# A chunked state scan in a decoder layer: the state's inputs are made by GpSimd from the scaled x instead of by VectorE from PSUM

## The chip, the core and the metric

The kernel runs on one core of a Trainium2 chip. The metric is the device time of one execution in microseconds (us). Three runs of the kernel before gave 635.28, 635.28 and 643.08 us, with a median of 635.28 us.

The engines are named as in the profile: PE is TensorE's matmul and PEld its weight load, DVE is VectorE, ACT is ScalarE, POOL is GpSimd, SP is the queue that issues DMAs.

## The reference, cut to what matters

A pre-norm decoder layer on x of shape 2 x 1024 x 256: a Mamba-2 block with a memory pool, then cross-attention, then a routed feed-forward with 8 experts. The change is inside the Mamba-2 scan, whose recurrence per head (8 heads of 64 columns, state width 128) is

```python
dt = jax.nn.softplus(dt + dt_bias)
A = -jnp.exp(A_log)
dA = jnp.exp(dt * A)
dtx = dt[..., None] * xs
def step(h, inp):
    dA_t, dtx_t, B_t, C_t = inp
    h = h * dA_t[:, :, None, None] + dtx_t[..., None] * B_t[:, None, None, :]
    y = jnp.einsum('bhpn,bn->bhp', h, C_t)
    return (h, y)
y = jnp.moveaxis(ys, 0, 1) + D_param[None, None, :, None] * xs
y = _rmsnorm(y * jax.nn.silu(z), gnorm_w)
```

## The kernel before, in words

The kernel is one program with five hand-written instruction streams, one for each engine. Each stream is in order, and the streams meet only at semaphores. The two batch rows make 2048 tokens, cut into 16 chunks of 128 tokens. Input projections, convolution and gates come first, then the scan over the 16 chunks, then scoring and the memory pool, cross-attention, and the experts.

The scan does not step token by token. For a chunk t it needs:

- G, the products of B and C inside the chunk (128 x 128), masked to the causal part: `gmat`;
- the decay between each pair of tokens for each head (128 x 8 x 128): ACT clamps and exponentiates it into `lmat`, and POOL multiplies it by G (`make_m`, L475, which signals `m_ready`);
- x scaled by dt, `xdt` (128 tokens x 512 columns), for the part of y that stays in the chunk (PE, L1760);
- x scaled by dt and by the decay to the chunk's end, `xend` (128 x 512), from which PE makes what the chunk adds to the state (L1764, into bank 6).

All of these have two buffers, picked by the parity p of the chunk. The steps of one chunk by stream, with t running from 1 to 14 in the steady part:

- PE, `pe_step(t)`: turns chunk t+1 from columns into rows with PE transposes into banks 0 and 1 (L1719 to L1721; it waits for `sides_ready`, since VectorE reads those banks), then `mix(t)`: the part of y from the earlier state (L1756; it waits for `state_added`), the part inside the chunk (L1760; it waits for `m_ready`), the addition to the state (L1764). Then it projects the gated y of chunk t-1 (L1775) and sums its squares (L1768).
- DVE, `dve_step(t)`: `chunk_sides(t+1)` copies B (L1166), masks G (L1169, signals `g_ready`), and makes `xdt` and `xend` from the same PSUM bank 0 (L1176, two instructions of one line; the second signals `sides_ready`). Then `sum_y(t)` (L1186, L1190), `add_state(t)` (L1195; it waits for PE's product and for POOL's decay), and `gate(t)`: four instructions that add D times x (L1200, both inputs in SBUF), and one that multiplies by the gate (L1207, both inputs in SBUF).
- POOL, `step(t)`: `decay_state(t)` multiplies the state by the chunk's decay (L484; it waits for `inter_mm` and `state_added`), `make_m(t+1)` (L475; waits for `decay_mat` and `g_ready`), `sum_squares(t-1)` (L489, L491).
- ACT: clamp (L697, eight instructions), exponential (L702), squares (L741), the residual (L753), and eviction of the output (L746, L748), each for its chunk.
- SP: for each chunk three loads: the chunk's columns (L367), the rows of cumulated decay (L373), the exponentials of those (L381).

Before the steady part DVE clamps chunk 0 and 1 itself (`clamp`, L1148). In the first `chunk_sides`, between `xdt` and `xend`, stand three more things: `clear_first` (L1153), the clamp of chunk 1, and `finish_decays`, which waits for ACT's last exponential (L737), clears entries of `dec` and multiplies `wend` by dt (L1158). ACT makes the exponential of `wend` in L736. PE's transposes of chunk 1 wait for `sides_ready` of chunk 0.

Of the kernel before, what the change touches and what calls it, by code (L numbers as in the profile page):

```python
# [10 lines left out]
ALU = mybir.AluOpType  # L11
ACT = mybir.ActivationFunctionType
AX = mybir.AxisListType.X
ds = bass.ds
# [9 lines left out]
DI, NS, H, HP = 512, 128, 8, 64  # L24
# [16 lines left out]
    "eps_set", "past_cleared", "ln_var_1", "rstd_1_1", "rstd_2_1", "rms_var_1", "rstd_3_1", "rstd_4_1",  # L41
    "ln_var_2", "rstd_1_2", "rstd_2_2", "rms_var_2", "rstd_3_2", "rstd_4_2", "dt_kept", "dt_steps_1",
    "dt_steps_2", "dt_abs", "dt_sum", "dt_ready", "cum_rows_kept", "cum_kept", "tot_kept", "wend_diff", "d_cols_set_1", "d_cols_set_2",
    "first_cleared_1", "first_cleared_2", "decay_ready", "gn_rstd_1", "ones_bf_set_1", "gn_rstd_2", "w2b_ready", "pos_ready", "cols_set", "mask_row_ready", "iotas_ready", "ln3_var", "ln3_rstd",
    "hot_ready", "prefix_ready", "held_ready", "block_expert_ready", "rows_found",
)
ACT_EVENTS = (
# [15 lines left out]
def events_of(name):  # L63
    return next(events for events in (DVE_EVENTS, ACT_EVENTS, POOL_EVENTS, PE_EVENTS) if name in events)


def at(name):

    return events_of(name).index(name) + 1


def build(nc, a, out):
# [3 lines left out]
    with ExitStack() as ctx:  # L76
# [5 lines left out]
        def sem(name):  # L82
            if name not in names:
                names[name] = ctx.enter_context(nc.semaphore(name))
            return names[name]


        dve_once, act_once, pool_once, pe_once = sem("dve_once"), sem("act_once"), sem("pool_once"), sem("pe_once")
        met = []

        def reached(name):
            met.append(name)
            events = events_of(name)
            assert [m for m in met if m in events] == list(events[:at(name)])
            return 1
# [18 lines left out]
        def cut(shape):  # L114
            n = int(np.prod(shape))
            v = arena[:, place[0]:place[0] + n]
            place[0] += n
            if len(shape) == 2:
                v = v.rearrange("p (a b) -> p a b", a=shape[0])
            if len(shape) == 3:  # L120
                v = v.rearrange("p (a b c) -> p a b c", a=shape[0], b=shape[1])
            return v
# [17 lines left out]
        xdt = cut([2, DI])  # L140
        xend = cut([2, DI])
# [32 lines left out]
        dt_v, dta, cum, dec = (dts[:, i, :] for i in range(4, 8))  # L174
        wend = dt_raw
        cum_rows, ecum_rows = dt_neg, dt_pos

        def th(v):
            return v.rearrange("p (t h) -> p t h", h=H)

        def heads(v, n):

            return v.unsqueeze(2).broadcast_to([P, H, n])
# [152 lines left out]
        S = sem  # L336
# [110 lines left out]
        def _(pool):  # L447
# [21 lines left out]
            pool.wait_ge(S("conv_done"), NX * NBLK)  # L469
            pool.memset(state, 0.0).then_inc(pool_once, reached("state_set"))  # L470

            def make_m(t, p):
                pool.wait_ge(S("decay_mat"), t + 1)
                pool.wait_ge(S("g_ready"), t + 1)
                pool.tensor_tensor(lmat[:, p, :, :], lmat[:, p, :, :],  # L475
                                   gmat[:, p, :].unsqueeze(1).broadcast_to([P, H, P]), ALU.mult
                                   ).then_inc(S("m_ready"), 1)

            def decay_state(t):

                pool.wait_ge(S("inter_mm"), t + 1)
                pool.wait_ge(S("state_added"), t)
                sv = state.rearrange("p (h n) -> p h n", h=H)
                pool.tensor_tensor(sv, sv, heads(dec[:, ds(t * H, H)], HP), ALU.mult).then_inc(S("state_decayed"), 1)  # L484

            def sum_squares(t, p):

                pool.wait_ge(S("sq_ready"), t + 1)
                pool.tensor_tensor(sq[:, p, 0:2, :], sq[:, p, 0:2, :], sq[:, p, 2:4, :], ALU.add).then_inc(S("sq_part"), 1)  # L489
                pool.wait_ge(S("sq_part"), t + 1)  # L490
                pool.tensor_tensor(sq[:, p, 0, :], sq[:, p, 0, :], sq[:, p, 1, :], ALU.add).then_inc(S("sq_summed"), 1)  # L491

            pool.wait_ge(pool_once, at("state_set"))
            make_m(0, 0)
            make_m(1, 1)
            pool.wait_ge(dve_once, at("first_cleared_2"))
            decay_state(0)

            def step(t, p):

                decay_state(t)
                make_m(t + 1, 1 - p)
                sum_squares(t - 1, 1 - p)
            step(1, 1)
            with pool.Fori(1, NT // 2 - 1) as i:
                step(2 * i, 0)
                step(2 * i + 1, 1)
# [70 lines left out]
            for n in range(NT // 2):  # L578
                pool.wait_ge(S("upd_ready"), n + 1)
                pool.wait_ge(S("res_y_added"), n + 1)  # L580
                xv = xres[:, 2 * n:2 * n + 2, :].rearrange("p a d -> p (a d)")
# [8 lines left out]
            with pool.Fori(0, NT // 2) as i:  # L590
                for p in range(2):
                    t = 2 * i + p
# [441 lines left out]
        def _(dve):  # L1034
# [110 lines left out]
            def clamp(t):  # L1145
                dve.wait_ge(S(f"cum_loaded{t}"), 16)
                for h in range(H):
                    i = dve.tensor_scalar(lmat[:, t, h, :], cum_all[:, t, h, :], cum[:, t * H + h:t * H + h + 1], 0.0, ALU.subtract, ALU.min)  # L1148
                i.then_inc(S("clamped"), 1)

            def clear_first():
                dve.wait_ge(act_once, at("ecum_exp"))
                dve.memset(ecum_rows[TB * H:TB * H + H, :], 0.0).then_inc(dve_once, reached("first_cleared_1"))  # L1153

            def finish_decays():
                dve.wait_ge(act_once, at("dec_exp"))
                dve.memset(th(dec)[:, 0:NT:TB, :], 0.0).then_inc(dve_once, reached("first_cleared_2"))
                dve.tensor_tensor(wend, wend, dt_v, ALU.mult).then_inc(dve_once, reached("decay_ready"))  # L1158
                dve.wait_ge(dve_once, at("decay_ready"))

            def chunk_sides(t, p, wait):

                dve.wait_ge(S("g_mm"), t + 1)
                if wait:
                    dve.wait_ge(S("state_mm"), t - 1)
                dve.tensor_copy(b_tok[:, p, :], bank[1][:, 0:P])  # L1166
                if wait:
                    dve.wait_ge(S("m_ready"), t - 1)
                dve.tensor_tensor(gmat[:, p, :], bank[1][:, P:2 * P], tri_le[:, :], ALU.mult).then_inc(S("g_ready"), 1)  # L1169
                xv = bank[0][:, :].rearrange("p (h n) -> p h n", h=H)  # L1170
                for dst, col in ((xdt, dt_v), (xend, wend)):
                    if dst is xend and isinstance(t, int) and t == 0:
                        clear_first()
                        clamp(1)
                        finish_decays()
                    i = dve.tensor_tensor(dst[:, p, :].rearrange("p (h n) -> p h n", h=H), xv, heads(col[:, ds(t * H, H)], HP), ALU.mult)  # L1176
                i.then_inc(S("sides_ready"), 1)

            def sum_y(t, p, first=False):
                yv = y_in[:, p, :, :]  # L1180
# [27 lines left out]

            clamp(0)
            chunk_sides(0, 0, False)  # L1210
            chunk_sides(1, 1, False)
            dve.wait_ge(S("conv_done"), NX * NBLK)
            sum_y(0, 0, True)
# [3 lines left out]
            def dve_step(t, p, wait=True):  # L1217
                chunk_sides(t + 1, 1 - p, True)
                sum_y(t, p)
                add_state(t)  # L1220
                gate(t, p, wait)
# [1044 lines left out]
```

## Time and profile before

| | |
|---|---|
| Runs | 635.28, 635.28, 643.08 us |
| Profiled execution: its own time, its span | 640.2 us, 638.5 us |
| PE busy | 584.8 us (92% of the span) |
| DVE busy | 393.2 us (62%) |
| ACT busy | 325.7 us (51%) |
| POOL busy | 171.6 us (27%) |
| Chain that ended last, by engine | PE 65%, DVE 19%, issue 7%, ACT 6% |

The profile comes from one execution of its own, with the time in the second row. Busy times are summed over the whole span. The chain that ended last is followed back from the last instruction, at each step to what released it. "Issue" is time for which the profile shows no wait. An engine's share over the whole span says little of one stage; the scan is the stretch from about 90 to 198 us.

### The profile page before, as it was taken

What the parts mean: (1) busy time and instruction counts of PE and PEld (TensorE: products, weight loads), DVE (VectorE), ACT (ScalarE), POOL (GpSimd) and SP (SyncE); (2) the same over time, 40 slices, a digit from 0 to 9 for tenths busy, and PEclk for the clock granted to TensorE, in tenths of its full rate; (3) what the DMA queues carried; (4) which work ended last, traced back from release to release, by engine and by line L of the source; (5) the groups of instructions that cost most, each with busy time, mean ns of one, the idle gap of its engine ahead of it and who ended that gap; (6) DMA issues with size and microseconds to landing.
All of it is one profiled execution on the core that took longest, in us unless ns stands there. A gap on an engine that the chain in (4) does not pass through costs nothing.

```text
span 638.5 us, 14059 instructions
## 1 busy us (share of the span) xinstructions
PE 584.8 (92%) x4820; PEld 462.1 (72%) x4821; DVE 393.2 (62%) x953; ACT 325.7 (51%) x708; POOL 171.6 (27%) x189
## 2 busy tenths in 40 slices
PE   7999998899988898987999999997599999999995
PEld 5444457677776565555788888886589999999994
DVE  4986798999997762555555566553744444444431
ACT  3887986777876413256566655554123322233220
POOL 0300016767673301741000000001212223322221
PEclk9999999999999679999999999998799999999998
DMA  8100126564532930008000000005711111111100
GB/s 257 43 1 0 46 81 191 151 193 156 169 127 78 394 136 4 1 1 263 12 19 11 18 18 19 10 18 126 247 26 35 34 32 31 35 40 34 28 17 0
DMA packets 47276, 49.50 MB, mean 78 GB/s; under 512 B 7607, under 2 KB 41627, under 8 KB 47227
## 3 DMA queue, kind: packets, MB, share of 16 engines
q1 hardware_dynamic: 41882, 43.65, 21.1%
q0 software_dynamic: 2208, 5.14, 2.9%
q8 instruction: 29, 0.48, 0.3%
q10 hardware_dynamic: 3136, 0.07, 0.3%
q14 instruction: 21, 0.16, 0.1%
HBM read 39.24 MB, written 5.26 MB: 70 GB/s over the span
## 4 chain that ended last, share of the span: by engine, by line
PE 65%; DVE 19%; issue 7%; ACT 6%; DVEq 1%; DMA 1%; POOL 1%; POOLq 0%; ACTq 0%
PE banks L2190 13%; PE banks L2201 12%; PE banks L1660 7%; DVE arena L1200 4%; PE banks L2043 4%; DVE arena L1176 3%; PE banks L2068 3%; PE banks L1944 3%; PE banks L2073 2%; PE banks L2086 2%; DVE arena L1125 2%; PE banks L2082 2%; PE banks L1955 2%; DVE ybuf L1417 2%; DVE arena L1186 1%
## 5 line engine op out<-in xcount | busy, mean ns | idle before, releaser
L1006 ACT ACTIVATE prob_b<-banks,gate_w 128x128 f32<-128x128 f32 x92 | 26.3, 368 | 115.5 <-PE banks L2190 115.5
L2201 PE MATMUL banks<-arena,prob_b 128*128 x368 | 83.1, 379 | 0.0
L2190 PE MATMUL banks<-ybuf 128*128 128x128 f32 x560 | 78.6, 275 | 0.0
L2201 PEld LDWEIGHTS banks<-arena,prob_b 128*128 128x128 f32 x368 | 68.2, 190 | 8.4
L2190 PEld LDWEIGHTS banks<-ybuf 128*128 128x128 f32 x560 | 72.1, 192 | 1.1
L1660 PE MATMUL banks<-featT,ybuf 128*128 128x512 f32 x160 | 70.2, 594 | 1.1 <-ACT featT L650 1.1
L1660 PEld LDWEIGHTS banks<-featT,ybuf 128*128 128x128 f32 x160 | 29.8, 190 | 36.6 <-issue 35.0
L1417 DVE TENSOR_REDUCE ybuf<-banks 128x12 f32<-128x1848 f32 (+1 forms) x32 | 46.1, 1441 | 15.7 <-PE banks L2043 15.7
L614 POOL DMA_INDIRECT out<-featT,dts x23 | 23.4, 1017 | 120.4 <-DVE featT L1606 120.4
L1125 DVE SCALAR_TENSOR_TENSOR arena<-arena,conv_w 128x512 f32<-128x512 f32 x72 | 48.9, 745 | 11.0 <-ACT arena L664 11.0
L594 POOL TENSOR_TENSOR xres<-xres,ybuf 128x256 f32 x16 | 11.6, 726 | 137.9 <-DVE ybuf L1437 137.9
L1584 DVE TENSOR_SCALAR prob_b<-banks,gate_w 128x128 f32<-128x128 f32 x92 | 26.0, 344 | 31.1 <-PE banks L2190 31.0
L475 POOL TENSOR_TENSOR arena<-arena 128x1024 f32<-128x1024 f32 x16 | 37.9, 2367 | 18.9 <-DVE arena L1169 10.3
L697 ACT ACTIVATE arena<-arena,dts 128x128 f32<-128x128 f32 x112 | 34.3, 389 | 6.5 <-DMA arena<-cum_rows 5.6
L2190 PE MATMUL banks<-ybuf,w_out 128*128 128x128 f32 x176 | 34.0, 275 | 0.0
L948 ACT ACTIVATE prob_b<-banks 122x2048 f32<-122x2048 f32 x16 | 30.1, 1879 | 7.1 <-PE banks L2068 7.1
L1775 PEld LDWEIGHTS banks<-w_out,arena 128*128 128x128 f32 x128 | 23.5, 190 | 12.8 <-DVE arena L1207 7.9
L1775 PE MATMUL banks<-w_out,arena 128*128 128x256 f32 x128 | 30.9, 384 | 1.6 <-DVE arena L1207 1.6
L1591 DVE COPY ybuf<-arena 128x1024 f32 x23 | 16.0, 697 | 26.6 <-PE banks L2190 25.3
L607 POOL DMA_INDIRECT xres<-x_rows,dts x23 | 23.8, 1034 | 23.9 <-DVEq L1564 17.2
L1423 DVE TENSOR_TENSOR arena<-arena,banks 128x512 f32<-128x512 f32 x16 | 11.0, 690 | 30.8 <-PE banks L2056 30.8
L2043 PE MATMUL banks<-arena 32*128 32x154 f32 x512 | 25.9, 314 | 4.4 <-DVE ybuf L1417 1.1
(354 smaller groups left out, 1240.1 us busy)
## 6 DMA issues: line engine op xcount, KB each, us to landing
arena<-cum_rows SPq DMA_DIRECT2D x16, 512.0 KB, 4.5
arena<-W1T SPq DMA_DIRECT2D x8, 1024.0 KB, 11.7
arena<-W2T SPq DMA_DIRECT2D x8, 1024.0 KB, 11.1
arena<-arena SPq DMA_DIRECT2D x16, 320.0 KB, 3.3
featT<-ecum_rows SPq DMA_DIRECT2D x30, 128.0 KB, 3.0
xres<-x SPq DMA_DIRECT2D x4, 512.0 KB, 11.2
x_rows<-xres SPq DMA_DIRECT2D x16, 128.0 KB, 2.2
ybuf<-attn_in_wT SPq DMA_DIRECT2D x1, 1288.0 KB, 7.0
```

The costliest lines, as they stand in the source:

```text
L475: pool.tensor_tensor(lmat[:, p, :, :], lmat[:, p, :, :], gmat[:, p, :].unsqueeze(1).broadcast_to([P, H, P]), ALU.mult).then_inc(S("m_ready ...
L697: i = act.activation(lmat[:, p, h, :], cum_all[:, p, h, :], ACT.Relu, bias=cum[:, ds(t * H + h, 1)], scale=-1.0)
L948: act.activation(prob_m[0:KM, :, :, :].rearrange("p h g n -> p h (g n)"), quad[0:KM, :, :], ACT.Exp).then_inc(S("prob_m_ready"), 1)
L1006: i = act.activation(hidT[:, p, f, :], bank[2 * p + 1][:, (f - 4) * P:(f - 3) * P], ACT.Relu, bias=b1_cols[:, ds(e * NFF + f, 1)])
L1125: i = dve.scalar_tensor_tensor(acc, raws[j][:, g, k:k + BLK], conv_w[:, g, k:k + 1], acc, ALU.mult, ALU.add)
L1417: dve.tensor_reduce(for_part.rearrange("p g h -> p h g"), quad[:, :, 0:n * LK].rearrange("p h (g n) -> p h g n", g=n), AX, ALU.max).then_i ...
L1584: i = dve.tensor_scalar(hidT[:, p, f, :], bank[2 * p][:, f * P:(f + 1) * P], b1_cols[:, ds(e * NFF + f, 1)], 0.0, ALU.add, ALU.max)
L1660: m = pe.matmul(in_bank(kind, n)[:, :], w_in[:, k, f * P:(f + 1) * P], featT[:, k, blk * BLK:(blk + 1) * BLK], start=(k == 0), stop=(k == ...
L1775: m = pe.matmul(bank[7][:, 0:D], gated[:, p, k, :], w_out[:, k, :], start=(k == 0), stop=(k == NZ - 1))
L2043: m = pe.matmul(quad[:, h, i * LK:(i + 1) * LK], qT[r, t % 3, g0 + i, :], keys[r, t // TB, g0 + i, :], start=True, stop=True)
L2190: m = pe.matmul(bank[2 * p + half][:, f * P:(f + 1) * P], w1_now[k][p][:, (4 * half + f) * P:(4 * half + f + 1) * P], xsT[:, p, k, :], sta ...
L2201: m = pe.matmul(bank[4 + p][:, 0:D], hidT[:, p, f, :], w2_of[:, ds(e * NFF + f, 1), :].rearrange("p a n -> p (a n)"), start=(f == 0), stop ...
```

## The change

`xend` is no longer made by VectorE. VectorE makes only `xdt` from PSUM, and signals `sides_ready` after it. GpSimd gets a new function `end_inputs(t, p)`, which multiplies `xdt` (SBUF) by `wend` (SBUF) into `xend`. So `wend` stays the bare decay, and the instruction that multiplied it by dt is gone. GpSimd's new instruction stands in its stream directly before `make_m` of the same chunk, and PE's product from `xend` keeps its place behind the wait for `m_ready`. In the first chunks the three things between `xdt` and `xend` now stand between `chunk_sides(0)` and `chunk_sides(1)`.

```diff
+            def end_inputs(t, p, wait=True):
+                pool.wait_ge(S("sides_ready"), t + 1)
+                if wait:
+                    pool.wait_ge(S("state_mm"), t - 1)
+                pool.tensor_tensor(xend[:, p, :].rearrange("p (h n) -> p h n", h=H), xdt[:, p, :].rearrange("p (h n) -> p h n", h=H),
+                                   heads(wend[:, ds(t * H, H)], HP), ALU.mult)
...
             pool.wait_ge(pool_once, at("state_set"))
+            pool.wait_ge(act_once, at("dec_exp"))
+            end_inputs(0, 0, False)
             make_m(0, 0)
+            end_inputs(1, 1, False)
             make_m(1, 1)
...
                 decay_state(t)
+                end_inputs(t + 1, 1 - p)
                 make_m(t + 1, 1 - p)
                 sum_squares(t - 1, 1 - p)
...
                 dve.memset(th(dec)[:, 0:NT:TB, :], 0.0).then_inc(dve_once, reached("first_cleared_2"))
-                dve.tensor_tensor(wend, wend, dt_v, ALU.mult).then_inc(dve_once, reached("decay_ready"))
-                dve.wait_ge(dve_once, at("decay_ready"))
...
-                for dst, col in ((xdt, dt_v), (xend, wend)):
-                    if dst is xend and isinstance(t, int) and t == 0:
-                        clear_first()
-                        clamp(1)
-                        finish_decays()
-                    i = dve.tensor_tensor(dst[:, p, :].rearrange("p (h n) -> p h n", h=H), xv, heads(col[:, ds(t * H, H)], HP), ALU.mult)
-                i.then_inc(S("sides_ready"), 1)
+                dve.tensor_tensor(xdt[:, p, :].rearrange("p (h n) -> p h n", h=H), xv, heads(dt_v[:, ds(t * H, H)], HP), ALU.mult
+                                  ).then_inc(S("sides_ready"), 1)
...
             chunk_sides(0, 0, False)
+            clear_first()
+            clamp(1)
+            finish_decays()
             chunk_sides(1, 1, False)
```

## Rows read from the trace of the kernel before

**Rows 1.** Stages view, the steady part; busy us and instructions of each engine, granted clock.

```profile
103.94:194.50 90.56, 82.13 (x605) 65.01 (x601) 86.05 (x169) 67.87 (x174) 66.09 (x56) 1.00 0.52 159
```

**Rows 2.** Chain of waits in the scan: start us, us, engine and line.

```profile
113.45 2.95 DVE arena L1200 x4
...
194.50 0.69 DVE arena L1186
```

**Rows 3.** Groups of POOL, steady part: idle before, with what ended it.

```profile
L475 POOL TENSOR_TENSOR arena<-arena 128x1024 f32<-128x1024 f32 x14 | 33.1, 2366 | 13.3 <-DVE arena L1169 7.5 <-ACT arena L702 5.8
L484 POOL TENSOR_TENSOR arena<-arena,dts 128x512 f32<-128x512 f32 x14 | 17.3, 1234 | 10.7 <-PE banks L1756 10.7
```

**Rows 4.** Timeline from 101.5 to 107.6 us, DVE: start us, us, line, count.

```profile
101.56 0.69 DVE L1195 TENSOR_TENSOR arena<-arena,banks 128x512 f32<-128x512 f32 x1 [1.09 <-POOL arena L484]
102.16 1.13 DVE L1200 SCALAR_TENSOR_TENSOR arena<-arena,d_cols 128x128 f32<-128x128 f32 x4
...
103.33 0.69 DVE L1207 TENSOR_TENSOR arena<-arena 128x512 f32<-128x512 f32 x1
103.94 0.28 DVE L1166 COPY arena<-banks 128x128 f32<-128x128 f32 x1
104.34 1.28 DVE L1176 TENSOR_TENSOR arena<-banks,dts 128x512 f32<-128x512 f32 x2
106.92 0.68 DVE L1195 TENSOR_TENSOR arena<-arena,banks 128x512 f32<-128x512 f32 x1
```

**Rows 5.** Timeline from 111.5 to 117.2 us, POOL and DVE.

```profile
111.54 2.37 POOL L475 TENSOR_TENSOR arena<-arena 128x1024 f32<-128x1024 f32 x1 [0.77 <-ACT arena L702]
113.37 3.02 DVE L1200 SCALAR_TENSOR_TENSOR arena<-arena,d_cols 128x128 f32<-128x128 f32 x4
113.87 0.79 POOL L489 TENSOR_TENSOR featT<-featT 128x256 f32<-128x256 f32 x1
114.73 0.46 POOL L491 TENSOR_TENSOR featT<-featT 128x128 f32<-128x128 f32 x1
115.15 1.10 POOL L484 TENSOR_TENSOR arena<-arena,dts 128x512 f32<-128x512 f32 x1
116.52 0.69 DVE L1207 TENSOR_TENSOR arena<-arena 128x512 f32<-128x512 f32 x1
```

**Rows 6.** Timeline, one clamp of chunk 1 on DVE and the POOL instruction beside it.

```profile
92.90 2.39 POOL L475 TENSOR_TENSOR arena<-arena 128x1024 f32<-128x1024 f32 x1 [2.88 <-ACT arena L702]
92.99 2.37 DVE L1148 TENSOR_SCALAR arena<-arena,dts 128x128 f32<-128x128 f32 x1
```

**Rows 7.** Timeline, two meetings of the gate multiply and the state's decay.

```profile
122.27 1.04 POOL L484 TENSOR_TENSOR arena<-arena,dts 128x512 f32<-128x512 f32 x1 [0.90 <-PE banks L1756]
122.29 1.57 DVE L1207 TENSOR_TENSOR arena<-arena 128x512 f32<-128x512 f32 x1 [0.24 <-DVE arena L1200]
...
128.94 0.69 DVE L1207 TENSOR_TENSOR arena<-arena 128x512 f32<-128x512 f32 x1 [0.24 <-DVE arena L1200]
128.94 1.59 POOL L484 TENSOR_TENSOR arena<-arena,dts 128x512 f32<-128x512 f32 x1 [0.92 <-PE banks L1756]
```

**Rows 8.** Timeline of the start of the scan: PE, DVE and POOL.

```profile
96.45 0.63 PE L1719 MATMUL banks<-ident,arena 128*128 128x128 f32 x4 [0.60 <-DVE arena L1176]
...
97.65 0.28 DVE L1169 TENSOR_TENSOR arena<-banks,tri_le 128x128 f32<-128x128 f32 x1
98.08 2.37 POOL L475 TENSOR_TENSOR arena<-arena 128x1024 f32<-128x1024 f32 x1 [2.80 <-DVE arena L1169]
100.39 1.06 POOL L484 TENSOR_TENSOR arena<-arena,dts 128x512 f32<-128x512 f32 x1
```

**Rows 9.** Waits of PE, 100 to 195 us: us in total, times, longest.

```profile
PE banks L1756 <- DVE arena L1195: 8.7, 10, 1.5
```

**Rows 10.** Stages view, two stretches after the scan, columns as in rows 1.

```profile
220.00:235.00 15.00, 14.22 (x69) 9.17 (x68) 8.13 (x36) 1.76 (x5) 0.00 (x0) 0.65 0.60 239
245.00:255.00 10.00, 7.55 (x45) 4.70 (x44) 1.21 (x5) 3.74 (x11) 2.56 (x14) 0.97 0.04 6
```

More of the change, by code:

```diff
@@ L43 @@
     "dt_steps_2", "dt_abs", "dt_sum", "dt_ready", "cum_rows_kept", "cum_kept", "tot_kept", "wend_diff", "d_cols_set_1", "d_cols_set_2",
-    "first_cleared_1", "first_cleared_2", "decay_ready", "gn_rstd_1", "ones_bf_set_1", "gn_rstd_2", "w2b_ready", "pos_ready", "cols_set", "mask_row_ready", "iotas_ready", "ln3_var", "ln3_rstd",
+    "first_cleared_1", "first_cleared_2", "gn_rstd_1", "ones_bf_set_1", "gn_rstd_2", "w2b_ready", "pos_ready", "cols_set", "mask_row_ready", "iotas_ready", "ln3_var", "ln3_rstd",
     "hot_ready", "prefix_ready", "held_ready", "block_expert_ready", "rows_found",
```

## The prediction

> **What bounds the kernel now.** I read the stages first, then the chain of waits through the scan, then the timeline of single chunks. In the steady part of the scan DVE is busy 86.05 of 90.56 us, PE 82.13, ACT 67.87 and POOL 66.09, at the full granted clock [rows 1]. The chain of waits runs through DVE's lines chunk after chunk [rows 2], and PE waits for DVE's add to the state 10 times, 8.7 us in all [rows 9]. So DVE sets the pace. The 14 frames from DVE's copy at 103.94 us [rows 4] to its instruction at 194.50 us [rows 2] take 90.56 us, 6.47 us each. A frame is DVE's work from one chunk's copy (L1166) to the next's.
>
> Busy time hides the next point: part of DVE's busy time is waiting inside an instruction. Take a frame with POOL out of the way, pieced together from rows 4. Copy to the scaled x is 104.34 - 103.94 = 0.40 us; copy to the add to the state (L1195) 106.92 - 103.94 = 2.98; that add to the first of the four skip instructions (L1200) 102.16 - 101.56 = 0.60; those four 103.33 - 102.16 = 1.17; the gate multiply (L1207) to the next copy 103.94 - 103.33 = 0.61. The sum is 2.98 + 0.60 + 1.17 + 0.61 = 5.36 us. Measured is 6.47, so 1.11 us a frame is lost to something, and DVE's recorded waits are too small to hold it.
>
> The timeline shows what it is lost to. The four L1200 take 3.02 us in one frame [rows 5] instead of 1.13 [rows 4], and their end follows POOL's instructions: POOL runs L475 until 113.91, L489 until 114.66, L491 until 115.19, L484 until 116.25, back to back, and the four end at 116.39, 0.14 us after the last. Between two POOL instructions one L1200 gets through, no more. Alone it is seen where a DVE clamp that begins 0.09 us after a POOL instruction takes 2.37 us and ends with it [rows 6]. Both directions occur [rows 7]: the gate multiply that starts 0.02 us after the state's decay takes 1.57 instead of 0.69 us; where both start together POOL takes 1.59 instead of 1.04 and DVE nothing extra. What reads PSUM is not held: the adds and products of PSUM with SBUF run in 0.68 us beside POOL in rows 4. So a DVE instruction with two SBUF inputs waits until the POOL instruction in progress is over.
>
> The SBUF — State Buffer page of the Trainium skill (section Who interferes with whom) says this outright: two SBUF inputs on DVE contend with GpSimd, the first holds the pair for its whole instruction, and at most one SBUF input does not contend. By that rule the new POOL instruction disturbs none of the PSUM steps beside it, and the sum below stays as it is; the trace agrees (0.68 us beside L475).
>
> **The change, part by part.**
>
> *DVE loses one instruction a frame.* The two L1176 become one; they take 1.28 us together and one alone 0.68 [rows 4], so DVE gains 0.60 us. All its later steps of the frame come 0.60 earlier: the first L1200 is ready 2.98 + 0.60 - 0.60 = 2.98 us after the copy.
>
> *POOL gets one instruction.* Nothing in the trace multiplies this very pair on POOL. The nearest is L484, the same shape and the same kind of broadcast column, 1.04 to 1.10 us where undisturbed [rows 5, 7, 8]; I take 1.06. Below it the bound is DVE's 0.68 for the same elements, above it 1.59, L484 held up. What reads PSUM on DVE lies beside it, so it isn't held. The GPSIMD Engine Reference of the Trainium skill (section 3.1) measures a two-input GpSimd multiply at 1.96 times DVE's; an estimate from it is 0.68 x 1.96 = 1.33 us, 0.27 more a frame, and the sum would be about 4 us higher. The row decides: 1.06.
>
> *The decay matrix product (L475) moves back.* This is what costs. Before, it waited for the masked G (end of L1169), or for ACT; from G's end to its start is 98.08 - 97.93 = 0.15 us [rows 8]. Now its queue holds the new instruction, which waits for the scaled x. In the new frame: scaled x ends at 0.40 + 0.68 = 1.08; the new instruction runs 1.23 to 2.29; L475 starts 0.06 before its forerunner's recorded end, as L484 does in rows 8, at 2.23, and with 2.37 us ends at 4.60. The first L1200 is ready at 2.98 and is held for 1.62 us. Before, with G's end at about 0.48, L475 could be over at about 3.0, and the first L1200 at 3.58 missed it.
>
> *After that every POOL instruction meets one L1200.* POOL's next three all have their inputs: the squares of the chunk before (that gate multiply ended at the frame's start), and the decay, which needs PE's product from the state (released by L1195 at about 3.1, over by about 4.6). So they run back to back as in rows 5. There, from L475's end to the gate multiply is 116.52 - 113.91 = 2.61 us. The gate multiply starts at 4.60 + 2.61 = 7.21, the next copy at 7.21 + 0.61 = 7.82 us. POOL waits for the next scaled x by then, so the frame repeats: its decay ends at about 7.0, and its next input comes at 7.82 + 1.23 = 9.05.
>
> *The sum of frames.* 14 x 7.82 = 109.5 us. In the last frame no decay follows the squares, and the last L1200 goes free: less 0.9. That leaves 108.6 against 90.56: +18.0 us.
>
> *The start.* PE's transposes of chunk 1 waited 0.60 us for DVE's second multiply of chunk 0 [rows 8]; that wait goes, and DVE's copy of chunk 1 comes 0.60 earlier, at 96.84. POOL then runs: new instruction 98.08 to 99.14 (scaled x ends at 97.93), L475 until 101.45, decay until 102.45. DVE's first add to the state waits for that decay already, 1.09 us [rows 4]; it now starts at about 102.56 instead of 101.56: +1.0 us. The new wait for ACT's last exponential and the product for chunk 0 lie ahead of chunk 1, and PE needs that product only after its own transposes; the deleted small multiply of `wend` and the clamp of chunk 1, which now runs before POOL is busy, are hidden by PE's weight products. I cost them at nothing; that cover is over 2 us of PE work, and if it were gone about 1 us would show.
>
> *Other queues.* Bank 0 comes free sooner, which PE can't use: it waits for L1195 in any case. On PE, chunk t+1's inside product starts after L475 at 4.6 instead of following the state's product at once, and its addition to the state ends near 6.8; DVE's next L1195 wants it at 7.82 + 2.38 = 10.2. ACT has 5.3 us of work in 7.82. SP's loads have more time than now. None becomes late.
>
> In all +18.0 + 1.0 = +19.0 us. Against the profiled execution's 640.2 that is 659.2; it stands 4.9 above the median, which I take as the base: 635.3 + 19.0 = **654 us**.
>
> **Rivals.**
>
> *DVE slips through.* The first L1200 gets its reads in before or within L475, or the new order leaves a gap. Then DVE keeps its 0.60 us and its old collisions: 6.47 - 0.60 = 5.87, near POOL's own work, 1.06 + 2.37 + 0.73 + 0.5 + 1.08 = 5.7. That gives 14 x -0.60 + 1.0 = -7.4 us, 628. For it: POOL is idle for 13.3 and 10.7 us before its two large instructions [rows 3], room for 14 new ones on paper. Against it: the meetings in [rows 5 to 7], where nothing got through. It decides if L475 ends before 2.98, so the new instruction would have to be no longer than zero. Chance 0.07.
>
> *Only the first L1200 is held.* It loses 1.62 us but the later ones lose no more than the old 1.11: 6.47 - 0.60 + 1.62 = 7.49 less the 0.4 or so that the decay took from the gate multiply, about 7.1. Then 14 x 0.63 + 1.0 = +9.8, 645, within 2%. For it: the decay sometimes starts with DVE [rows 7]. Against it: with L1195 far ahead, the decay isn't waiting for PE. Chance 0.12.
>
> *PE's clock falls.* PE idles about 1.2 us a frame more. The granted clock was 0.65 in a stretch where half was spent at 1.2 GHz, but 0.97 in one with PE busy 7.55 of 10 us [rows 10]; the new scan would have it busy 5.87 of 7.82, the same 75%. At the lower level 5.87 us of PE work a frame would be up to 11.7; three or four such frames add some 14 us: 668. Chance 0.06.
>
> **How the numbers follow.** Forecast 0.75. Its own range is 647 to 661: 14 frames with the new instruction at 0.68 (-5) or at 1.33 to 1.59 (+4 to +7), and the base between the runs. The range that holds 8 in 10 takes in most of the second rival below and something of the clock above: 644 to 664. Differences under 2%, 12.7 us, can't be told from no change here. Slower by over that (above 648): most of the forecast and all of the clock's case, 0.78; within: 0.18; faster: 0.04, as the first rival's 628 is itself within 2% and only its lower end is not.
>
> **What would show it.** A frame of about 7.8 us on DVE; L1200 at about 1.0 us an instruction (the four take some 4.1 us); POOL's new line at about 1.06 us; L475 starting about 2.2 us after DVE's copy; L484 no longer waiting for PE. It is wrong if L475 is over before the first L1200 starts, if L1200 runs in 0.35 us while L475 is in progress, or if PE's granted clock in the scan is under 1.

## The result, and the profile after

The kernel after takes 655.46 us (median of 4 runs, 653.38 to 657.43), against 635.28 us before. The ratio is 1.0307, 95% interval 1.0265 to 1.0349: 3.1% slower. The forecast was 654 us.

The profiled execution took 653.38 us, with a span of 651.6 us. The stages view of its steady part, with the columns of [rows 1], and the part after the scan:

```profile
105.15:214.31 109.16, 88.60 (x612) 66.65 (x610) 102.45 (x156) 67.90 (x174) 78.48 (x70) 0.98 0.42 126
214.31:651.60 437.29, 400.77 (x3868) 342.33 (x3868) 227.71 (x601) 178.57 (x382) 92.20 (x114) 0.97 0.19 62
```

The same 14 frames now take 109.16 us instead of 90.56 [rows 1]: +18.6. They begin at 105.15 instead of 103.94 us: +1.2. The scan thus ends 19.8 us later, close to the difference of the medians, 20.2 us. (The two spans differ by 13.1 only. The rest is after the scan: 437.29 us here, 444.00 before, with the same instructions at a mean granted clock of 0.97 against 0.96.)

Groups of the steady part, DVE then POOL; L1204 is now the skip instructions, L1211 the gate multiply, L1180 the scaled x, L476 the new multiply, L482 the decay matrix product, L491 the state's decay, L496 and L498 the sums of squares:

```profile
L1204 DVE SCALAR_TENSOR_TENSOR arena<-arena,d_cols 128x128 f32<-128x128 f32 x56 | 50.5, 960 | 0.0
L1180 DVE TENSOR_TENSOR arena<-banks,dts 128x512 f32<-128x512 f32 x14 | 9.5, 679 | 0.0
```

```profile
L482 POOL TENSOR_TENSOR arena<-arena 128x1024 f32<-128x1024 f32 x14 | 33.0, 2357 | 0.0
L491 POOL TENSOR_TENSOR arena<-arena,dts 128x512 f32<-128x512 f32 x14 | 15.2, 1082 | 6.6 <-PE banks L1763 5.2 <-issue 1.4
L476 POOL TENSOR_TENSOR arena<-arena,dts 128x512 f32<-128x512 f32 x14 | 14.6, 1042 | 24.2 <-DVE arena L1180 24.2
```

DVE is busy 102.45 us, 16.4 more, though it has one instruction a frame less. The 56 skip instructions are 50.5 us of it, 0.96 us each; free they take 0.35. POOL's two waits of [rows 3] have become one: 24.2 us ahead of L476, for the scaled x. L482 never waits. L491 still waits for PE, but only in the first two frames, 5.2 us in all.

One steady frame, DVE and then POOL, start and length in us:

```profile
121.01 0.28 DVE L1175 COPY arena<-banks 128x128 f32<-128x128 f32 x1
121.41 0.68 DVE L1180 TENSOR_TENSOR arena<-banks,dts 128x512 f32<-128x512 f32 x1
123.40 0.68 DVE L1199 TENSOR_TENSOR arena<-arena,banks 128x512 f32<-128x512 f32 x1
124.00 3.32 DVE L1204 SCALAR_TENSOR_TENSOR arena<-arena,d_cols 128x128 f32<-128x128 f32 x4
127.56 1.48 DVE L1211 TENSOR_TENSOR arena<-arena 128x512 f32<-128x512 f32 x1 [0.24 <-DVE arena L1204]
128.97 0.28 DVE L1175 COPY arena<-banks 128x128 f32<-128x128 f32 x1
```

```profile
122.27 1.04 POOL L476 TENSOR_TENSOR arena<-arena,dts 128x512 f32<-128x512 f32 x1 [2.15 <-DVE arena L1180]
123.28 2.36 POOL L482 TENSOR_TENSOR arena<-arena 128x1024 f32<-128x1024 f32 x1
125.59 0.78 POOL L496 TENSOR_TENSOR featT<-featT 128x256 f32<-128x256 f32 x1
126.45 0.46 POOL L498 TENSOR_TENSOR featT<-featT 128x128 f32<-128x128 f32 x1
127.45 1.04 POOL L491 TENSOR_TENSOR arena<-arena,dts 128x512 f32<-128x512 f32 x1 [0.55 <-issue]
```

L482 starts 2.27 us after the copy and ends at 125.64. The first skip instruction of that frame by itself:

```profile
124.00 1.78 DVE L1204 SCALAR_TENSOR_TENSOR arena<-arena,d_cols 128x128 f32<-128x128 f32 x1
```

It starts at 124.00, is ready to work for 1.64 us while L482 runs, and ends at 125.78, 0.14 us after it. The frame closes at 7.96 us; in this one the gate multiply, not the last skip instruction, is what meets L491. Over 13 frames, copy to copy, the mean is 7.86 us against 6.49 before.

### The profile page after: what moved, and what is told of

Read it like the earlier page. It is cut to its first block, busy times and chain, and to the rows that moved or that the text cites. A ratio compares the mean times of both kernels' runs of the same rounds, so it can differ in the third digit from the quotient of the medians.

```text
span 651.6 us, 14073 instructions
## 1 busy us (share of the span) xinstructions
PE 586.7 (90%) x4820; PEld 461.5 (71%) x4821; DVE 405.9 (62%) x936; ACT 326.1 (50%) x708; POOL 185.4 (28%) x205
## 4 chain that ended last, share of the span: by engine, by line
PE 62%; DVE 18%; ACT 8%; issue 7%; POOL 2%; DMA 1%; DVEq 1%; POOLq 0%; ACTq 0%
PE banks L2197 13%; PE banks L2208 12%; DVE arena L1204 8%; PE banks L1667 7%; PE banks L2050 4%; PE banks L2075 3%; PE banks L2080 2%; PE banks L2093 2%; PE banks L2089 2%; PE banks L1962 2%; PE banks L1951 2%; DVE ybuf L1424 2%; DVE arena L1190 1%; ACT arena L687 1%; DVE arena L1180 1%
## 5 line engine op out<-in xcount | busy, mean ns | idle before, releaser
L1204 DVE SCALAR_TENSOR_TENSOR arena<-arena,d_cols 128x128 f32<-128x128 f32 x64 | 53.0, 887 | 0.0
L482 POOL TENSOR_TENSOR arena<-arena 128x1024 f32<-128x1024 f32 x16 | 37.7, 2356 | 0.0
## 6 DMA issues: line engine op xcount, KB each, us to landing
xres<-x SPq DMA_DIRECT2D x4, 512.0 KB, 10.7
```

Source lines behind the costliest of these rows:

```text
L482: pool.tensor_tensor(lmat[:, p, :, :], lmat[:, p, :, :], gmat[:, p, :].unsqueeze(1).broadcast_to([P, H, P]), ALU.mult).then_inc(S("m_ready ...
L1204: i = dve.scalar_tensor_tensor(y_in[:, p, k, :], xbcT[:, k, ds(t * P, P)], d_cols[:, k:k + 1], y_in[:, p, k, :], ALU.mult, ALU.add)
```

## The experiments

**The theories.** *Lock*: a DVE instruction with two SBUF inputs is held until the POOL instruction in progress is over, so the order and timing of POOL's instructions against DVE's skip and gate instructions set the frame. *Occupancy*: POOL has too much to do. *Late product*: the decay matrix product comes late, and DVE waits through PE. For each kernel the frame below is the mean from copy to copy over the same 13 frames (the third copy to the sixteenth) of its profiled execution.

**1. The new multiply alone taken out.** PE makes the addition to the state from `xdt`, so the decay to the chunk's end is left out of the result.

```diff
 (kernel after)
-                end_inputs(t + 1, 1 - p)
                 make_m(t + 1, 1 - p)
...
-                    pe.matmul(bank[6][:, :], b_tok[:, p, :], xend[:, p, :], start=True, stop=True).then_inc(S("state_mm"), 1)
+                    pe.matmul(bank[6][:, :], b_tok[:, p, :], xdt[:, p, :], start=True, stop=True).then_inc(S("state_mm"), 1)
```

> The kernel after without GpSimd's new multiply; PE makes the chunk's addition to the state from the scaled x, so the decay to the chunk's end is left out. VectorE still has its one multiply less. The lock theory (a DVE instruction with two SBUF inputs is held until POOL's instruction in progress is over; the new multiply pushes the decay matrix product in front of the skip instructions): the product is back at about 0.6 us after the copy and over at 3.0, so the skip instructions lose only to the squares; frames of about 6.0 us, time 626 to 631 us, below the kernel before. The late-product theory (the product's lateness delays PE, and DVE waits for PE) gives the same here. If instead something else in the new order costs (the earlier signal, the clamp moved, the start), it stays above 645 us.

Measured: 635.68 us, ratio to before 0.9983 (0.9951 to 1.0015), frame 6.60 us. So the multiply on POOL carries the whole 20 us; the moved clamp, the earlier signal and the start carry none of it. But the gain I expected from DVE's missing multiply isn't there either. Its frame, DVE and POOL:

```profile
150.24 0.28 DVE L1172 COPY arena<-banks 128x128 f32<-128x128 f32 x1
153.22 2.77 DVE L1201 SCALAR_TENSOR_TENSOR arena<-arena,d_cols 128x128 f32<-128x128 f32 x4
156.23 0.69 DVE L1208 TENSOR_TENSOR arena<-arena 128x512 f32<-128x512 f32 x1 [0.24 <-DVE arena L1201]
```

```profile
153.19 0.73 POOL L496 TENSOR_TENSOR featT<-featT 128x256 f32<-128x256 f32 x1
154.00 0.46 POOL L498 TENSOR_TENSOR featT<-featT 128x128 f32<-128x128 f32 x1
154.80 1.04 POOL L491 TENSOR_TENSOR arena<-arena,dts 128x512 f32<-128x512 f32 x1 [0.35 <-PE banks L1760]
```

The skip instructions start 0.60 us earlier in the frame, and thereby meet the whole of L496, L498 and L491: 2.77 us for four. I had let the fourth pass before the decay. Over the 13 frames the skip and gate instructions, in the kernel before and here:

```profile
L1200 DVE SCALAR_TENSOR_TENSOR arena<-arena,d_cols 128x128 f32<-128x128 f32 x52 | 22.1, 484 | 0.0
L1207 DVE TENSOR_TENSOR arena<-arena 128x512 f32<-128x512 f32 x14 | 14.6, 1040 | 2.8 <-DVE arena L1200 2.6
```

```profile
L1201 DVE SCALAR_TENSOR_TENSOR arena<-arena,d_cols 128x128 f32<-128x128 f32 x52 | 35.7, 745 | 0.0
L1208 DVE TENSOR_TENSOR arena<-arena 128x512 f32<-128x512 f32 x14 | 10.2, 729 | 2.8 <-DVE arena L1201 2.6
```

(The 14th gate multiply is the undisturbed one, 0.69 us, that ends just behind the first copy.) A frame has 1.05 us more in the skip instructions, 0.34 less in the gate multiply and 0.60 less in the multiply that is gone: 0.11 us longer, as measured. The 0.60 us saved on DVE came back as holding.

**2. The skip and gate instructions read PSUM, in the kernel before.** The running sum stays in the bank of the inside product, so that each of these DVE instructions has one SBUF input.

```diff
 (kernel before)
-                dve.tensor_tensor(yv, yv, INTRA_BANK[p]..., ALU.add)
+                dve.tensor_tensor(sums, yv, sums, ALU.add)          # sums = INTRA_BANK[p], PSUM
...
-                    i = dve.scalar_tensor_tensor(y_in[:, p, k, :], xbcT[...], d_cols[:, k:k + 1], y_in[:, p, k, :],
+                    i = dve.scalar_tensor_tensor(sums[:, k, :], xbcT[...], d_cols[:, k:k + 1], sums[:, k, :],
...
-                dve.tensor_tensor(gated[:, p, :, :], y_in[:, p, :, :], zsT[...], ALU.mult)
+                dve.tensor_tensor(gated[:, p, :, :], sums, zsT[...], ALU.mult)
```

> The kernel before, with the skip and gate instructions of VectorE reading their running sum from PSUM (it stays in the bank of the inside product, in place) instead of SBUF, so that none of them has two SBUF inputs. Same instructions, same counts, same waits. Lock theory: the skip instructions never wait for POOL; the 1.11 us a frame goes, the four take about 1.2 us, and the frame comes down to PE's 5.9 us or so: 14 x -0.5 = -7 us, 625 to 631 us. Theories without a lock (POOL's occupancy, plain memory bandwidth): no change or slightly slower from PSUM access, 635 to 640 us.

Measured: 621.92 us, ratio 0.9788 (0.9732 to 0.9843), frame 5.53 us.

```profile
156.88 0.68 DVE L1196 TENSOR_TENSOR arena<-arena,banks 128x512 f32<-128x512 f32 x1
157.47 1.12 DVE L1202 SCALAR_TENSOR_TENSOR banks<-arena,d_cols,banks 128x128 f32<-128x128 f32 x4
158.84 0.69 DVE L1209 TENSOR_TENSOR arena<-banks,arena 128x512 f32<-128x512 f32 x1 [0.24 <-DVE banks L1202]
```

```profile
156.80 2.36 POOL L475 TENSOR_TENSOR arena<-arena 128x1024 f32<-128x1024 f32 x1 [0.68 <-ACT arena L702]
```

Four skip instructions run in 1.12 us while POOL's 2.36 us product is in progress. That is no faster than the 1.13 us that they take from SBUF with POOL out of the way [rows 4]; PSUM takes nothing off their work, only the holding is gone. Its median is the lowest of this study, and the gain is larger than I expected, since I had put PE's floor at 5.9 us from busy times that include waiting.

**3. The same edit in the kernel after.**

```diff
 (kernel after)
-                dve.tensor_tensor(gated[:, p, :, :], y_in[:, p, :, :], zsT[...], ALU.mult)
+                dve.tensor_tensor(gated[:, p, :, :], sums, zsT[...], ALU.mult)
... and the other two edits of experiment 2
```

> The kernel after with the same change of the skip and gate instructions to PSUM. Lock theory: the frame falls from 7.9 to about 5.9 us, bounded by PE and by POOL's own 5.7 us of work: 14 x -2.0 = -28 us, 625 to 631 us. Late-product theory: the decay matrix product still ends 4.6 us after the copy, so if DVE or PE truly waited for it the time stays near 650 us. Occupancy theory: POOL's work is the same, frame stays near 7.9 us, 655 us.

Measured: 624.03 us, ratio 0.9823 (0.978 to 0.9866), frame 5.54 us. Against the kernel after that is 31 us, from an edit that leaves POOL's instructions and their order as they were. In the stages view of its scan PE is busy all the time, and POOL nearly so:

```profile
105.00:183.00 78.00, 77.92 (x591) 64.00 (x587) 66.57 (x156) 66.01 (x174) 75.16 (x68) 1.00 0.57 175
```

POOL gets the new multiply and all else done in 5.5 us a frame: occupancy does not explain 7.86. Nor does the late product: here it comes later still (in the frame from the copy at 148.90 us it starts at 152.72 and ends at 155.08, 6.18 us after the copy), and in the kernel after PE waited for it 3.7 us in all of the scan, at most 0.3 at a time. And with the holding gone, before and after have the same frame, 5.53 and 5.54: over the 13 frames PE is busy 71.93 of 71.93 us and 72.04 of 72.04, so PE sets it, and DVE's saved 0.60 us is worth nothing.

**4. The new multiply behind the product instead of ahead.**

```diff
 (kernel after; the multiply signals end_ready; the same order for chunks 0 and 1)
-                end_inputs(t + 1, 1 - p)
                 make_m(t + 1, 1 - p)
+                end_inputs(t + 1, 1 - p)
...
+                    pe.wait_ge(S("end_ready"), t + 1)
                     pe.matmul(bank[6][:, :], b_tok[:, p, :], xend[:, p, :], start=True, stop=True).then_inc(S("state_mm"), 1)
```

> The kernel after with GpSimd's new multiply behind the decay matrix product of the same chunk instead of ahead of it, with a signal of its own that PE waits for before the addition to the state. POOL does the same work. Lock theory: the product is over 3.0 us after the copy, one skip instruction slips in behind it, the others meet the new multiply and the squares, the gate multiply meets the state's decay: frame about 6.9 us, 14 x -1.0, 638 to 645 us. Occupancy theory: as the kernel after, 655 us.

Measured: 648.11 us, ratio 1.0211 (1.0162 to 1.0261), frame 7.27 us. The order is worth 7.3 us, with the same POOL work, and PE's new wait never shows in the profile. But the frame is 0.4 above my figure, and the time above my range. In this frame the skip instructions meet everything that POOL still has to do:

```profile
158.58 3.47 DVE L1204 SCALAR_TENSOR_TENSOR arena<-arena,d_cols 128x128 f32<-128x128 f32 x4
162.29 0.69 DVE L1211 TENSOR_TENSOR arena<-arena 128x512 f32<-128x512 f32 x1 [0.24 <-DVE arena L1204]
```

```profile
158.53 1.04 POOL L476 TENSOR_TENSOR arena<-arena,dts 128x512 f32<-128x512 f32 x1
159.53 0.78 POOL L496 TENSOR_TENSOR featT<-featT 128x256 f32<-128x256 f32 x1
160.39 0.46 POOL L498 TENSOR_TENSOR featT<-featT 128x128 f32<-128x128 f32 x1
160.81 1.09 POOL L491 TENSOR_TENSOR arena<-arena,dts 128x512 f32<-128x512 f32 x1
```

None slipped in between L482 and L476 here: L476 started at 158.53, 0.05 us before the first skip instruction. Four POOL instructions held four skip instructions, 3.47 us.

**5. More of the multiply.** A second one, over 6 of 8 heads, ahead of the new one.

```diff
 (kernel after; spare is an unused buffer)
+                pool.tensor_tensor(spare[:, p, :]..., xdt[:, p, 0:6 * HP]..., wend[:, ds(t * H, 6)]..., ALU.mult)
                 pool.tensor_tensor(xend[:, p, :]..., xdt[:, p, :]..., heads(wend[:, ds(t * H, H)], HP), ALU.mult)
```

> The kernel after with one more GpSimd multiply of the same kind ahead of the new one, over 6 of the 8 heads (128x384) into a spare buffer; about 0.8 us, between the 0.73 us of the 128x256 sum and the 1.04 us of the 128x512 multiply. Lock theory: nothing else in the frame waits, so every frame grows by just those 0.8 us, from 7.8 to 8.6, all of it inside the first skip instruction: 14 x 0.8 = +11 us against the kernel after, 664 to 669 us. Occupancy theory (POOL short of time): POOL still idles over 2 us a frame in the kernel after, so it would absorb it: 655 us.

Measured: 665.53 us, ratio to before 1.0474 (1.0417 to 1.053), frame 8.38 us: +0.52 a frame and +10 us. POOL idled 1.63 us a frame ahead of the pair, against 1.73 ahead of the one multiply in the kernel after, and so absorbed almost none of it. The frame grew by less than the instruction's 0.83 us, because the product now starts so late that the first skip instruction gets in just ahead of it:

```profile
150.89 3.97 DVE L1208 SCALAR_TENSOR_TENSOR arena<-arena,d_cols 128x128 f32<-128x128 f32 x4
```

```profile
150.96 2.49 POOL L486 TENSOR_TENSOR arena<-arena 128x1024 f32<-128x1024 f32 x1
```

The skip instruction began 0.07 us before the product, and the product took 2.49 instead of 2.36 us: the 0.13 us is POOL's turn to be held.

**6. The skip instructions alone moved to PSUM, in the kernel before.**

```diff
 (kernel before; the gate multiply still reads y_in and zsT from SBUF)
-                    i = dve.scalar_tensor_tensor(y_in[:, p, k, :], xbcT[...], d_cols[:, k:k + 1], y_in[:, p, k, :],
+                    i = dve.scalar_tensor_tensor(y_in[:, p, k, :], xbcT[...], d_cols[:, k:k + 1], sums[:, k, :],
```

> The kernel before with only the four skip instructions reading their running sum from PSUM; the gate multiply keeps two SBUF inputs. Lock theory: the skip instructions are never held (1.1 to 1.2 us for four); the gate multiply meets the state's decay in some frames and is held up to 1.0 us there: frames between 5.6 and 6.5 us, mean about 6.0, 626 to 632 us. If only the gate multiply mattered the time would stay at 636 us.

Measured: 625.39 us, ratio 0.9851 (0.9796 to 0.9905), frame 5.68 us, just faster than expected: the gate multiply, 0.82 us on average, is mostly first and holds the second sum of squares instead (L491 in this kernel, 0.67 us on average where it takes 0.46). So taking the holding off the skip instructions brings 0.81 of the 0.95 us a frame that experiment 2 won. Not all of it was lost in them: by the rows of experiment 1 the kernel before held the four for 0.57 us a frame (1.70 less the free 1.13) and the gate multiply for 0.38 (1.07 less 0.69). Once the skip instructions end earlier, the gate multiply mostly misses the state's decay too.

**7 and 8. A filler on POOL behind the product, in the kernel before: a memset, and a copy onto itself, both 128x768.**

```diff
 (kernel before, ahead of the sums of squares; the other kernel has pool.memset(filler, 0.0))
+                pool.tensor_copy(filler, filler)
```

> The kernel before with a filler on GpSimd ahead of the sums of squares, right behind the decay matrix product: a memset of 128x768, which writes SBUF and reads nothing. Beside it the skip instructions start. If only GpSimd's reads hold a DVE instruction with two SBUF inputs, the skip instructions run in 0.35 us beside the memset, and the frame grows by 0 to 0.5 us through the later squares; if any GpSimd instruction holds them, it is as long as with the copy.

> The same filler place with a copy of 128x768 onto itself, which reads and writes SBUF. It holds one skip instruction for its whole length; the squares and the decay behind it hold the other three: the frame grows by its length, about 0.8 to 1.2 us, 14 frames, 647 to 653 us.

Measured, two runs each: 643.86 us with the memset, ratio 1.0142 (1.0071 to 1.0213), 0.74 us long, frame 7.14; 643.33 with the copy, ratio 1.0134 (1.0058 to 1.021), 0.82 us long, frame 7.01. The two are alike, and both grew by less than I expected of the copy, since the decay after them had waited for PE anyway: 10.7 us in 14 frames before, 3.3 with the copy. Whether a memset holds DVE the times don't tell, as in most frames the skip instructions became ready only at its end. One frame of each has a skip instruction that becomes ready in the middle of the filler (L491 in these two kernels):

```profile
108.46 0.75 POOL L491 MEMSET arena<- 128x768 f32 x1
108.80 0.35 DVE L1204 SCALAR_TENSOR_TENSOR arena<-arena,d_cols 128x128 f32<-128x128 f32 x1
```

```profile
107.66 0.82 POOL L491 COPY arena<-arena 128x768 f32<-128x768 f32 x1
107.99 0.64 DVE L1204 SCALAR_TENSOR_TENSOR arena<-arena,d_cols 128x128 f32<-128x128 f32 x1
```

Beside the memset it ran free and was over before the memset; beside the copy it was held and ended 0.15 us after it. That speaks for reads alone holding DVE, but it is one meeting of each kind, so this stays open.

## Why the prediction was right

**DVE sets the pace, and 1.11 us of its frame is holding.** Right in kind, a little too large: the holding is 0.95 us (0.57 in the skip instructions, 0.38 in the gate multiply), and the frame falls by as much, to 5.53, when it is taken out (experiment 2). The free frame was put together as 5.36 from a frame without the 0.24 us that DVE waits ahead of the gate multiply in 11 of the 13 frames; experiment 2 still has that wait.

**DVE loses 0.60 us.** Right as a count: L1180 has 9.5 us where the two had 17.9. Worth nothing by itself (experiment 1), and nothing once the holding is gone (experiment 3).

**The new multiply takes 1.06 us.** Measured 1.04. The 1.33 us estimated from the GPSIMD Engine Reference of the Trainium skill (section 3.1) did not come; the page's ratio is that of an add of 2048 elements, not of a multiply as the prediction has it, and the row of the same shape and broadcast was the better guide.

**The product moves to 2.23 us after the copy and ends at 4.60; the first skip instruction is held 1.62 us.** Measured 2.27, 4.63 and 1.64 in the frame shown. This is the step on which the forecast rests, and experiments 1, 4 and 5 each move the product's place in the frame, the first and the last with POOL's work, the fourth without.

**The frame.** Forecast 7.82, measured 7.86 (7.47 to 8.39). The way from the product's end to the next copy, 3.22 us by [rows 5], is 3.33 in the frame shown; there the decay held the gate multiply instead of the last skip instruction. The steady frames mostly go by turns: in one the four skip instructions take 4.1 us, as forecast, and the frame 7.93; in the next they take 3.3 and the gate multiply 1.21, and the frame 7.68. The forecast had only the first kind.

**The start costs 1.0 us.** Measured 1.2. DVE's add waited for POOL's decay, as forecast, and started at 102.77 us where the forecast had 102.56. What I gave a chance of 0.06 did happen there for a moment: in this execution PE was busy 3.25 of 6 us at the start, and its granted clock fell to its lower level, 1.2 GHz, for some 7 us. (The prediction took 0.65 in a stretch for half of it at 1.2 GHz; it is 70%.) Stages view of 100 to 106, 106 to 110 and 110 to 114 us:

```profile
100.00:106.00 6.00, 3.25 (x20) 2.86 (x20) 3.19 (x9) 4.23 (x11) 2.93 (x3) 0.76 0.64 190
106.00:110.00 4.00, 4.00 (x20) 2.55 (x17) 1.92 (x4) 0.39 (x1) 4.00 (x3) 0.51 0.22 64
110.00:114.00 4.00, 4.00 (x38) 3.63 (x37) 3.97 (x10) 2.43 (x9) 1.81 (x4) 1.00 0.63 214
```

DVE waited for PE 0.77 and 1.31 us in the first frame and 0.23 in the second. But in the first its skip instructions came so late by those waits that they took only 1.77 us, so that this frame, 7.47 us, was the shortest of the 13. That the sum of 14 came out at 109.16 against a forecast of 108.6 is partly luck: a wait that the forecast did not have was made good by holding that did not come. One of the signs that I gave for being wrong, a granted clock under 1 in the scan, did show (0.98 in the 14 frames), but it cost next to nothing. From 121 us on the clock is full, with PE at 68.50 of 86.26 us.

**The rivals.** "DVE slips through" fell with the first skip instruction of every steady frame. "Only the first is held": the four take 3.2 to 4.4 us in every frame but the first, where 1.78 and the three free ones, about 0.8, would make 2.6.

**What was right for a weak reason.** I put PE's floor at 5.9 us a frame from its busy time. It is 5.5: the same matmuls fill a frame of 5.53 in experiment 2, so some of the busy time before was not work. In the kernel after this floor was never reached, so it did no harm; in the expectations it made me undersell experiments 2 and 3.

## What to carry to other kernels

Before moving elementwise work from VectorE to GpSimd, list VectorE's instructions with two SBUF inputs and lay GpSimd's instructions over them in time. An engine with idle time can still be the wrong place: what counts is which VectorE instruction each of its instructions will hold, and what it pushes back in its own queue. Better still, remove the meeting: let a running sum stay in PSUM, so that VectorE has one input there; here that was worth 14 us before the change and 31 us after it, with no instruction added or removed.

## What the runs showed of the hardware

- Holding is in whole instructions, in both directions: DVE's 128x128 instruction took 1.78 us beside the rest of a 2.36 us product, and a product that began 0.07 us after it took 2.49 us.
- When POOL's instructions follow each other at once, one DVE instruction gets through between two of them: four skip instructions against three or four POOL instructions, 2.77 us (experiment 1) and 3.47 us (experiment 4).
- DVE's 128x128 multiply-add in place in PSUM costs the same as in SBUF: 1.12 and 1.13 us for four.
- I had not expected that a saving on DVE could be given back in full: 0.60 us a frame less work, and the frame went from 6.49 to 6.60 us, as the skip instructions were held for 1.05 us a frame more (experiment 1).
